# Field 23's last tile of rows fetched by ScalarE, and the first chunk numbers spread by TensorE

## The reference

```python
B, N_DENSE, N_FIELDS, VOCAB, EMBED_DIM, ATT_DIM = (2048, 13, 26, 12500, 32, 8)
FIRST, SECOND = np.triu_indices(N_FIELDS, k=1)
emb = jax.vmap(lambda tbl, idx: tbl[idx], in_axes=(0, 1), out_axes=1)(embed_tables, sparse)
bi = emb[:, FIRST, :] * emb[:, SECOND, :]
a = jax.nn.relu(jnp.einsum('bpd,dh->bph', bi, att_w_w) + att_w_b)
scores = jnp.einsum('bph,ho->bpo', a, att_d_w) + att_d_b
att_weight = jax.nn.softmax(scores, axis=1)
att_out = jnp.sum(att_weight * bi, axis=1)
x = jnp.concatenate([att_out, dense], axis=-1)
out = jax.nn.sigmoid(x @ fin_w + fin_b)
```

## Time and profile before

| | us |
|---|---|
| median of 3 runs | 484.43 |
| lowest, highest | 483.49, 484.66 |
| the profiled execution's own time | 483.39 |
| its span, first to last instruction | 481.6 |
| TensorE matmul busy | 450.2 (93%) |
| VectorE busy | 372.6 (77%) |
| GpSimd busy | 347.9 (72%), 368 gathers |
| ScalarE busy | 95.8 (20%) |
| granted TensorE clock, mean | 0.996 of full |

### The profile page before, as it was taken

One profiled execution on the slowest core, in us unless ns is written; L12 is line 12 of the kernel. 1 busy time (PEld: TensorE's weight loads), 2 busy tenths in 40 slices (PEclk: granted clock), 3 DMA queues, 4 the chain that ended last, 5 costly groups with the idle time before them and its releaser, 6 DMA issues.

```text
span 481.6 us, 6198 instructions
## 1 busy us (share of the span) xinstructions
PE 450.2 (93%) x2280; PEld 177.6 (37%) x2280; DVE 372.6 (77%) x645; ACT 95.8 (20%) x198; POOL 347.9 (72%) x372
## 2 busy tenths in 40 slices
PE   0699999999998999999999899999999899999884
PEld 0354443343333533333333443333334344333221
DVE  6337788796965979799775969879786788887985
ACT  0000101131252011112243101113234201114253
POOL 5777777777777777777777777777777777777740
PEclk9999999999999999999999999999999999999998
DMA  6933743121122223222112222213111222322210
GB/s 221 250 13 15 147 58 36 13 15 13 15 13 15 14 14 79 15 14 14 14 14 13 15 13 15 13 13 15 14 13 16 14 15 13 15 13 14 15 10 1
DMA packets 13661, 15.06 MB, mean 31 GB/s; under 512 B 6368, under 2 KB 12608, under 8 KB 13248
## 3 DMA queue, kind: packets, MB, share of 16 engines
q0 software_dynamic: 11776, 6.05, 23.1%
q1 hardware_dynamic: 1360, 7.53, 4.2%
q10 hardware_dynamic: 496, 1.09, 0.6%
HBM read 14.61 MB, written 0.03 MB: 30 GB/s over the span
## 4 chain that ended last, share of the span: by engine, by line
PE 78%; POOL 8%; DVE 5%; issue 4%; DMA 3%; ACT 1%; POOLq 0%; DVEq 0%
PE looked_own L391 33%; PE back_s L391 16%; PE first L405 13%; PE sums_f L415 12%; POOL emb L368 8%; PE sums_s L429 3%; DVE onehot L667 2%; DMA chunk_numbers<-index_chunk 1%; DMA emb<-tables,rows 1%; DMA chunk_of<-chunk_numbers 1%; PE back_f L442 1%; PE back_s L452 1%; DVE look_masked L678 1%; DMA par<-params 1%; DVE ring L691 0%
## 5 line engine op out<-in xcount | busy, mean ns | idle before, releaser
L368 POOL DMA_INDIRECT emb<-tables,rows x324 | 305.9, 944 | 98.7 <-issue 96.9
L691 DVE TENSOR_TENSOR ring<-emb_t,turned 128x512 f32<-128x512 f32 (+9 forms) x180 | 193.9, 1114 | 3.4
L391 PE MATMUL looked_own<-look_table,onehot 128*128 128x448 f32 x434 | 178.0, 554 | 17.0 <-DVE onehot L667 16.7
L391 PEld LDWEIGHTS looked_own<-look_table,onehot 128*128 128x128 f32 x434 | 79.5, 192 | 114.4 <-issue 114.4
L507 ACT ACTIVATE hidden<-first,par 128x512 f32<-128x512 f32 (+1 forms) x84 | 56.5, 678 | 284.7 <-PE first L405 284.4
L391 PE MATMUL back_s<-look_table,onehot 128*128 128x448 f32 x238 | 94.4, 545 | 3.1 <-DVE score L739 3.1
L405 PE MATMUL first<-ring,par 128*32 128x512 f32 (+1 forms) x672 | 90.7, 591 | 4.3 <-DVE ring L691 4.3
L415 PE MATMUL sums_f<-ring,par 128*32 128x512 f32 (+1 forms) x672 | 90.0, 583 | 0.0
L667 DVE TENSOR_TENSOR onehot<-chunk_of,turned 128x2048 f32<-128x2048 f32 (+1 forms) x24 | 48.3, 2018 | 26.6 <-PE looked_own L391 21.2
L391 PEld LDWEIGHTS back_s<-look_table,onehot 128*128 128x128 f32 x238 | 44.0, 190 | 51.7 <-issue 51.7
L368 POOL DMA_INDIRECT emb<-tables,rows_first x44 | 41.8, 950 | 17.2 <-issue 13.1
(11 more groups left out here) (56 smaller groups left out, 101.0 us busy)
## 6 DMA issues: line engine op xcount, KB each, us to landing
emb<-tables,rows POOLq DMA_INDIRECT x324, 3.2
look_table<-tables SPq DMA_DIRECT2D x3, 1568.0 KB, 8.2
chunk_of<-chunk_numbers SPq DMA_DIRECT2D x3, 768.0 KB, 4.9
chunk_of<-chunk_numbers ACTq DMA_DIRECT2D x1, 768.0 KB, 3.8
emb<-tables,rows_first POOLq DMA_INDIRECT x44, 3.8
par<-params ACTq DMA_DIRECT2D x1, 258.5 KB, 3.1
ids<-sparse SPq DMA_DIRECT2D x1, 208.0 KB, 2.5
feats<-dense SPq DMA_DIRECT2D x1, 104.0 KB, 8.1
```

Of the source, the lines that this page charges most:

```text
L368: pool.indirect_dma_start(emb[:, f, g * D:(g + 1) * D], None, stacked, bass.IndirectOffsetOnAxis(ap=row, axis=0),).then_inc(gathered[f], 16)
L391: mm = nc.tensor.matmul(looked_rows[look_bank[tile]], onehot[:, c, g * P:(g + 1) * P], look_table[:, n, c, :], start=c == 0, stop=c == CHU ...
L691: nc.vector.tensor_tensor(slot[:, at:at + n, :], emb_t[:, i:i + n, :], turned[:, f % 2, :].unsqueeze(1).broadcast_to((P, n, P)), ALU.mult) ...
```

## The change

It has two parts. **Rows.** Field 23 is gathered by GpSimd for three tiles of each quad, not four. The fourth tile's 128 rows come by 128 DMAs on ScalarE's queue, one row of 32 floats each, into one partition each. ScalarE issues 8 of them ahead of the work of each of the fields 0 to 15. The row numbers come on partition 0 to 3 (one per quad) in `row_ids`; VectorE clamps them into `row_numbers`, and ScalarE loads 16 at a time into registers. VectorE waits for `rows_fetched` before it transposes field 23. From the second quad on ScalarE waits ahead of the first row until field 23 of the quad before has been transposed.

**Chunk numbers.** For quad 0 and look-up field 3, TensorE multiplies `index_chunk` with a broadcast column of the identity (four matmuls into the bank `first[0]`), which puts each number on all partitions. VectorE makes the two first one-hots from that bank, ahead of the rest of its preparation, and compares with the parameters' own copy of the chunk numbers. The DRAM way stays for the other numbers. The first table is loaded in two pieces with a semaphore each, the second table right behind it and not after `chunk_of`; `feats` goes from SP's queue to ScalarE's. Scratch tiles move into `final`.

```diff
+ROW_FIELD = 23
+ROWS_LOADED = 16
+ROWS_BESIDE = 8
+ROWS_BESIDE_FIELDS = range(16)
...
-        return G
+        return G - 1 if f == ROW_FIELD else G
...
+        chunk_first = first[0][:, 0:G * P]
...
+            sp.dma_start(row_ids[:], row_index).then_inc(row_ids_in, 16)
...
+                if n == 0:
+                    sp.dma_start(look_table[:, n, STEPS[0]], rows_n[:, STEPS[0]]).then_inc(look_table_first_in, 16)
+                    sp.dma_start(look_table[:, n, STEPS[1]], rows_n[:, STEPS[1]]).then_inc(look_table_in[n], 16)
+                else:
+                    sp.dma_start(look_table[:, n], rows_n).then_inc(look_table_in[n], 16)
...
             load_table(0)
-            sp.dma_start(feats[:], dense.rearrange("(p t) n -> p t n", t=T)).then_inc(feats_in, 16)
-            sp.wait_ge(chunk_of_in[0], 16)
             load_table(1)
+            sp.wait_ge(chunk_numbers_home, 16)
             load_chunks(1)
...
+            pe.wait_ge(index_chunk_made, 1)
+            for g in range(G):
+                row = ident[0:QUADS * LOOKS * G, g:g + 1].broadcast_to((QUADS * LOOKS * G, P))
+                mm = nc.tensor.matmul(chunk_first[:, g * P:(g + 1) * P], row, index_chunk[:], start=True, stop=True)
+            mm.then_inc(chunk_first_spread, 1)
...
-                    pe.wait_ge(look_table_in[n], 16)
+                    pe.wait_ge(look_table_first_in if n == 0 and part == 0 else look_table_in[n], 16)
...
+                def fetch_rows(f):
+                    at = ROWS_BESIDE_FIELDS.index(f) * ROWS_BESIDE
+                    if at == 0 and q == 0:
+                        act.wait_ge(row_numbers_ready, 1)
+                    if at == 0 and q:
+                        act.wait_ge(transposed, (q - 1) * F + ROW_FIELD + 1)
+                    if at % ROWS_LOADED == 0:
+                        _, numbers[:] = nc.values_load_multi_w_load_instructions(
+                            row_numbers[q:q + 1, at:at + ROWS_LOADED], engines=(mybir.EngineType.Activation,), min_val=0,
+                            max_val=F * V - 1, skip_runtime_bounds_check_because="rows are clamped to their table")
+                    for p in range(at, at + ROWS_BESIDE):
+                        act.dma_start(emb[p:p + 1, ROW_FIELD, (G - 1) * D:], stacked[bass.ds(numbers[p % ROWS_LOADED], 1), :]
+                                      ).then_inc(rows_fetched, 16)
...
+                fetch_rows(0)
                 for f in range(1, F):
+                    if f in ROWS_BESIDE_FIELDS:
+                        fetch_rows(f)
                     done = groups_of(f)
                     for gr in done:
                         relu_group(gr)
...
+                if of == 0 and n == 0:
+                    dve.wait_ge(chunk_first_spread, 1)
+                    numbers, here = chunk_first[:, tiles], par[:, cols["look_chunk"]]
...
+            make_onehots(0, 0, 0)
+            make_onehots(0, 0, 1)
 
             dve.wait_ge(rows_first_ready, 1)
             make_rows(3, T, F, rows, rows_ready)
...
+            dve.wait_ge(row_ids_in, 16)
+            nc.vector.tensor_scalar(row_clamped, row_ids[:], float(-V), float(V - 1), ALU.max, ALU.min
+                                    ).then_inc(row_steps, 1)
...
+                    if f == ROW_FIELD:
+                        dve.wait_ge(rows_fetched, (q + 1) * (16 * P))
```

More of the change, by code:

```diff
@@ L36, in layout, with attention_fm @@
     return cols, at
-def attention_fm(nc, dense, sparse, tables, params, look_index, chunk_numbers, out):
+def attention_fm(nc, dense, sparse, tables, params, look_index, row_index, chunk_numbers, out):
     f32, i32 = mybir.dt.float32, mybir.dt.int32
@@ L118, in gathers_of @@
             return G - LOOK_TILES[LOOK.index(f)]
-        return G
+        return G - 1 if f == ROW_FIELD else G
+    assert ROW_FIELD not in LOOK and ROWS_BESIDE * len(ROWS_BESIDE_FIELDS) == P and ROWS_LOADED % ROWS_BESIDE == 0
+    assert ROWS_BESIDE_FIELDS[-1] < ROW_FIELD
     assert G * D == P and B % (P * G) == 0 and RING < GROUPS and 1 < END_GROUPS
@@ L211, in attention_fm @@
             "p (t f) -> p t f", f=F) for i in range(2))
+        row_clamped, row_wrap = (final[0:QUADS].rearrange("p g e -> p (g e)")[:, i * P:(i + 1) * P] for i in range(2))
+        index_clamped, index_wrap, index_part = (
+            final[0:QUADS * LOOKS * G].rearrange("p g e -> p (g e)")[:, G * P + i * P:G * P + (i + 1) * P] for i in range(3))
         neg_max = sb("neg_max", [P, G])
@@ L251, in attention_fm @@
         rows_ready = sem("rows_ready")
+        row_ids_in = sem("row_ids_in")
+        row_steps = sem("row_steps")
+        row_numbers_ready = sem("row_numbers_ready")
+        rows_fetched = sem("rows_fetched")
         gathered = [sem(f"gathered{f}") for f in range(F)]
@@ L254, in attention_fm @@
         look_table_in = [sem(f"look_table_in{n}") for n in range(len(LOOK))]
+        look_table_first_in = sem("look_table_first_in")
+        chunk_first_spread = sem("chunk_first_spread")
         index_in = sem("index_in")
@@ L316, in pairs_of, with chunk_numbers_of @@
             return cut.rearrange("p g (e c j) -> p e g c j", c=PAIRS_C, j=COL_TILES)
-        def chunk_numbers_of(q):
-            return chunk_numbers[q:q + 1].broadcast_to((P, LOOKS * G * P))
+        def chunk_numbers_of(q, n=0):
+            return chunk_numbers[q:q + 1, n * G * P:].broadcast_to((P, (LOOKS - n) * G * P))
         block = ctx.enter_context(nc.Block())
@@ L492, in _ @@
             act.dma_start(par[:, rest], params[:, rest]).then_inc(par_in, 16)
+            act.dma_start(feats[:], dense.rearrange("(p t) n -> p t n", t=T)).then_inc(feats_in, 16)
             act.wait_ge(index_chunk_made, 1)
@@ L497, in _ @@
             act.wait_ge(chunk_numbers_home, 16)
-            act.dma_start(chunk_of[:, 0].rearrange("p n b -> p (n b)"), chunk_numbers_of(0)).then_inc(chunk_of_in[0], 16)
+            act.dma_start(chunk_of[:, 0, 1:].rearrange("p n b -> p (n b)"), chunk_numbers_of(0, 1)
+                          ).then_inc(chunk_of_in[0], 16)
             act.wait_ge(par_in, 16)
@@ L543, in exponentiate_early @@
                                              accum_out=early[:, 0, g:g + 1]).then_inc(early_exp_done, 1)
+                def fetch_rows(f):
[11 more added lines that the diff above has]
+                                      ).then_inc(rows_fetched, 16)
+                numbers = []
+                stacked = tables.rearrange("f v d -> (f v) d")
+                fetch_rows(0)
                 for f in range(1, F):
+                    if f in ROWS_BESIDE_FIELDS:
+                        fetch_rows(f)
                     done = groups_of(f)
@@ L606, in _, with make_onehots @@
                                     ).then_inc(index_chunk_made, 1)
+            dve.wait_ge(par_in, 16)
+            def make_onehots(of, n, part):
+                tiles, chunks = slice((G - LOOK_TILES[n]) * P, G * P), STEPS[part]
+                numbers, here = chunk_of[:, of % 2, n, tiles], chunk_here
+                if of == 0 and n == 0:
+                    dve.wait_ge(chunk_first_spread, 1)
+                    numbers, here = chunk_first[:, tiles], par[:, cols["look_chunk"]]
+                else:
+                    dve.wait_ge(chunk_of_in[of % 2], (of // 2 + 1) * 16)
+                    dve.wait_ge(looked, first_step(of, n) - len(STEPS) + part + 1)
+                shape = (P, chunks.stop - chunks.start, LOOK_TILES[n] * P)
+                nc.vector.tensor_tensor(onehot[:, chunks, tiles], numbers.unsqueeze(1).broadcast_to(shape),
+                                        here[:, chunks].unsqueeze(2).broadcast_to(shape), ALU.is_equal
+                                        ).then_inc(onehot_made, 1)
+            make_onehots(0, 0, 0)
+            make_onehots(0, 0, 1)
             dve.wait_ge(rows_first_ready, 1)
@@ L635, in _ @@
             dve.wait_ge(chunk_here_made, 1)
+            dve.wait_ge(row_ids_in, 16)
+            nc.vector.tensor_scalar(row_clamped, row_ids[:], float(-V), float(V - 1), ALU.max, ALU.min
+                                    ).then_inc(row_steps, 1)
+            dve.wait_ge(row_steps, 1)
+            nc.vector.tensor_scalar(row_wrap, row_clamped, 0.0, float(V), ALU.is_lt, ALU.mult).then_inc(row_steps, 1)
+            dve.wait_ge(row_steps, 2)
+            nc.vector.scalar_tensor_tensor(row_numbers[:], row_clamped, float(ROW_FIELD * V), row_wrap, ALU.add, ALU.add
+                                           ).then_inc(row_numbers_ready, 1)
             dve.wait_ge(feats_in, 16)
@@ L658, in turn_field @@
                     tr.then_inc(transposed, 1)
[L660 to L670, removed]
                 def take_looked(tile):
@@ L699, in _ @@
                     for i in steps_beside(q, 0):
-                        for of, n, part in onehots_for([i]):
-                            make_onehots(of, n, part)
                         for tile in tiles_ended([i - 1] if i else []):
@@ L834 @@
```

(1 more changed line is left out.)

11 lines of the change are left out of this document (4 added, 7 removed).

## The result

| | before | after |
|---|---|---|
| median, us | 484.55 (483.49 to 484.75, 4 runs) | 493.40 (490.94 to 493.72, 4 runs) |
| ratio, with its 95% interval | | 1.0175 (1.0144 to 1.0206) |
| profiled execution, its span | 483.39, 481.6 | 493.72, 491.5 |
| TensorE busy, granted clock | 450.2, 0.996 | 458.5, 0.986 |
| GpSimd busy, gathers | 347.9, 368 | 345.0, 364 |

What follows compares the result with a forecast made beforehand. TensorE was taken to bound the first three quads, the end hanging on two nearly level strands. TensorE's -6.5 - 1.8 + 3.2 = -5.1 and GpSimd's -5.0 gave -5.0 us from 484.43: 479.4 us, range 478.2 to 481.5.

Steps and rivals of the forecast that it cites:

- GpSimd's strand: GpSimd's run of gathers to the kernel's end: four gathers fewer, 5.0 us earlier, a ceiling on the whole gain.
- The rival of the stretched period: On GpSimd, 512 more DMAs stretch the gathers' period by 1.1%, eating the 5.0 us: 484.4 us; chance 0.05.
- Two level strands: At the kernel's end GpSimd's strand and TensorE's strand are nearly level; a gain needs both to shrink.
- ScalarE's stall: TensorE waiting for late relus ahead of the score products: 1.1 us in each of quads 1 to 3, 3.2 in all.
- The opening: Start of quad 0: TensorE spreads the chunk numbers, so its look-ups start 6.5 us earlier, near 9.7.
- the bound of 6.0: In the opening, the lead if the first table piece took as long as the whole load: 6.0 us.
- Where the stall falls: In quads 1, 2 and 3, the score products needing relu 3 behind 96 rows are the narrow place; quad 0 has time.
- c: Time one row holds ScalarE's queue, everything included: taken as 0.44 us, lower bound 0.34, upper 1.25.
- The formula: Stall ahead of the score products in each of quads 1, 2 and 3: 96 c - 41.16 us.
- The limit between faster and slower: On ScalarE's queue, the value of c from which its lateness decides the sign: 0.458, only 0.02 above the value taken.
- TensorE's strand: TensorE's and VectorE's work to the kernel's end: -6.5 at the start, -1.8 at the end, +3.2 of stalls, -5.1 us.
- The rival's 496.6: ScalarE late for the score products, c = 0.50: 6.8 us in each of three quads, 496.6 us; chance 0.35.

Runs made afterwards that it cites:

- e4d_sp_rows: The changed kernel with its row DMAs and the loads of their numbers issued by SyncE, not ScalarE: 478.68 us, ratio 0.9899 to the kernel before.

## Why the prediction was wrong

- **GpSimd's strand, -5.0: right, within 1 us.** 364 gathers; with SyncE's rows the last starts at 458.20, with ScalarE's and with one DMA per quad at 458.6 to 459.2. Those up to 1.0 us are not explained: the list of waits has no new one of that size. The rival of the stretched period is refuted, since with the same 512 transfers on SyncE it is (458.20 - 4.50) / 363 = 1.250 us as before; in the changed kernel it is 1.252, where that rival needed 1.264.
- **Two level strands: right in the half that was measured.** The opening alone gives 0, both with SyncE's rows -5.0. This is the sum of the forecast without ScalarE's stall, and the 479.49, 478.68 and 479.47 of three kernels stand where 479.4 was forecast.
- **The opening, -6.5: mis-sized.** It gave 5.05. The four spreading matmuls took 2.04 us and not 1.4, the one-hot started at 8.03 and not 7.3, and the first look-up tile took 0.84 us longer. Its first weight loads come 0.75 us apart and the later ones 0.375, so TensorE starts at half pace; in the changed kernel the step to full pace is at 16.6 us, with the opening alone already at 14.3, where the tile took 7.28 us and the lead was 6.3. I had no term for when that step falls. Even the bound of 6.0 was too high. Where ScalarE is in time GpSimd's strand is the ceiling, and this cost nothing; in the changed kernel it is 1.5 us of the miss.
- **Where the stall falls: right, with one place missed.** The score products wait for relu 3 behind 96 rows. I had put limits to relus 0, 3 and 6 only; relus 1 and 2, behind 72 and 88 rows, were late too, 1.91 and 0.76 us. Before the change, the first products that need them start at 189.83 and 197.14, so their limit was c = 0.458 each. The formula itself holds: from the start of the row DMAs at 151.14 to relu 3 at 197.22 are 46.1 us, or 0.480 for a row (the first load had run beside the exponentials; with it the row costs 0.49 to 0.50), and 96 x 0.480 - 41.16 = 4.9, where the score products came 5.0, 5.3 and 5.0 us late. Quad 0 showed no stall, as said.
- **The size of c, 0.44: this is the step that failed.** I took ScalarE's own issues of 0.44 from start to start as nearest and let "a sixteenth of a load" disappear in it, with no row for the load's length. The issue was cheaper (0.39), the load 1.29 us, and the first DMA behind it 0.23 us longer: 1.52 / 16 = 0.095 us on each row. With 0.44 a quad loses 1.1 us by the formula, with 0.48 4.9. The limit between faster and slower was 0.458, and I saw that it was near, but gave the far side 0.35. The section "Why a DMA increments its semaphore by 16 and not by 1" of the Trainium skill's "DMA: Bandwidth & Descriptors" I had read as a one-row DMA holding the sequencer longer than one of 128 partitions. The measured 0.235 us against 0.34 goes against that reading; "Rules for kernel authors" of the same page of the Trainium skill, to coalesce small transfers, was the better guide.
- **The clock: missing from the sum.** A stall of TensorE was counted by its length. In each of quads 1, 2 and 3 the granted clock fell to 0.50 for some 3 us, but only in quad 1 did that cost anything. There it fell at the last wait, and the 1.5 us came on top: 5.0 + 1.5 of the quad's 6.5. In quads 2 and 3 it was down behind the first of the two waits (the stretches from 307 to 309 and 427 to 429 us stand at 0.50), and the slower products only shortened the wait for relu 3, whose time ScalarE's queue sets: the quads lost 5.3 and 5.0, no more than the score products were late.
- **The miss in one sum.** TensorE's strand was to end 5.1 us earlier and ended 9.9 later, a miss of 15.0: three stalls of 15.3 and not 3.2 are 12.1, the opening is 1.5, the clock 1.5. The rival's 496.6 was for c = 0.50 in every row; the formula got 0.480.
- **The range.** Its upper end of 481.5 does not follow from "c up to 0.45": that gives 96 x 0.45 - 41.16 = 2.0 in each of three quads, and 484.4 - 8.3 + 6.1 = 482.2. The result lies far above either.

## What to carry to other kernels

Work given to an "idle" engine costs by what stands behind it in its queue: 128 rows fit easily into ScalarE's idle time and still made it late, the same rows one or two fields further on, or on SyncE, cost nothing. Where one price decides the sign, every instruction of the new chain needs a row or a bound of its own, the register loads above all. And when two strands are level, shortening one gives nothing: one edit alone reads as useless, although it is half of the gain (shown here for TensorE's strand, argued for GpSimd's).

## What the runs showed of the hardware

- Loading 16 numbers into registers took 1.29 us on ScalarE and 1.23 on SyncE, 32 took 2.22 on ScalarE. The first DMA behind a load took 0.47 us on ScalarE in place of 0.235, and 0.26 in place of 0.225 on SyncE (e4d_sp_rows, at 153.9).
- ScalarE's sequencer ran ahead of its engine: the load ahead of quad 1's rows started at 149.8, while the exponentials went on to 151.1, and rows were issued 0.14 us after a relu of 0.69 us had started.
- TensorE's first look-up matmuls ran at half pace (0.75 us apart, then 0.375) in each of the seven kernels profiled at 477 to 492 us, for 4 to 6 us, though the granted clock of those stretches stands at 1.00 in the windows.
- In the changed kernel TensorE's granted clock stood at 0.50 for some 3 us behind waits of 1.91, 0.76 and 2.00 us in quad 1, and behind a single one of 2.27 and of 2.19 us in quads 2 and 3. With 32 numbers per load the longest wait in those quads was 1.98 us, and it stayed at 1.00 (at 302 to 310 us).
